# A scaled copy moved from ScalarE to GpSimd in the second of four serial scans, and a reordered tail

## The reference

```python
def step(prev, cur):
    new = cur + jax.nn.relu(_row_conv(prev, K))   # 9 taps along the row, 64 -> 64 channels
    return (new, new)
y = _dir_scan(y, k_td, reverse=False)
y = _dir_scan(y, k_dt, reverse=True)
yt = jnp.swapaxes(y, 1, 2)
yt = _dir_scan(yt, k_lr, reverse=False)
yt = _dir_scan(yt, k_rl, reverse=True)
```

## Time and profile before

| | |
|---|---|
| median of 3 runs | 705.79 us (705.42 to 707.0) |
| the profiled execution | 706.54 us |
| its span, first to last instruction | 704.7 us |
| mean granted clock of TensorE | 0.974 of full speed |
| TensorE busy, matmuls | 636.4 us, 90% |
| VectorE busy | 570.4 us, 81% |
| ScalarE busy | 462.6 us, 66% |
| GpSimd busy | 140.8 us, 20% |
| second scan | 120.6 to 237.0 us of the span |
| attention and tail | from 451 us on |

### The profile page before, as it was taken

How to read it: one execution, slowest core, us unless ns; L and a number is a source line. 1 busy time by engine, 2 the same in 40 slices (tenths; PEclk the granted TensorE clock), 3 DMA queues, 4 the chain that set the end, 5 groups by cost and what they waited for, 6 DMA issues and landing times.

```text
span 704.7 us, 27312 instructions
## 1 busy us (share of the span) xinstructions
PE 636.4 (90%) x10484; PEld 538.4 (76%) x10484; DVE 570.4 (81%) x1943; ACT 462.6 (66%) x1061; POOL 140.8 (20%) x115
## 2 busy tenths in 40 slices
PE   4999999999999899999999999698888898898960
PEld 4899999898888899999999999556454464554530
DVE  4899998888888798989999999897595686785682
ACT  3555666999999666666666666574666676676531
POOL 0023000000000000000000000000627658549363
PEclk9999999999999999999999999889999999999995
DMA  9999850000000000000000000002342835835756
GB/s 175 203 201 198 166 108 1 1 0 0 0 0 0 1 2 0 0 0 0 1 1 0 0 0 0 0 2 60 71 106 57 171 85 104 178 74 122 159 87 120
DMA packets 63611, 43.27 MB, mean 61 GB/s; under 512 B 42000, under 2 KB 56144, under 8 KB 63568
## 3 DMA queue, kind: packets, MB, share of 16 engines
q1 hardware_dynamic: 60272, 41.89, 30.1%
q10 hardware_dynamic: 3296, 0.82, 0.6%
HBM read 33.39 MB, written 9.31 MB: 61 GB/s over the span
## 4 chain that ended last, share of the span: by engine, by line
DVE 31%; PE 26%; issue 17%; POOL 12%; ACT 7%; DMA 3%; DVEq 1%; ACTq 1%; POOLq 0%; SPq 0%
PE bank L468 20%; DVE scan_rows L735 9%; POOL rows_h L395 9%; DVE parts L721 8%; DVE parts L735 7%; DVE fin L794 3%; ACT cols_w L1077 3%; POOL fin L424 2%; DMA rows_h<-bounce 2%; ACT parts L1061 2%; DVEq L735 1%; PE bank L597 1%; DMA yn<-L_conv_k_td 1%; PE bank L518 1%; PE bank L544 1%
## 5 line engine op out<-in xcount | busy, mean ns | idle before, releaser
L468 PE MATMUL bank<-parts 128*128 128x124 f16 (+2 forms) x7560 | 433.5, 219 | 16.1 <-DVE parts L236 8.7
L468 PEld LDWEIGHTS bank<-parts 128*128 128x128 f16 x7560 | 417.7, 98 | 31.8 <-issue 12.0
L1061 ACT ACTIVATE parts<-parts 128x128 f16<-128x128 f16 x508 | 157.1, 309 | 125.9 <-DVE parts L735 104.3
L721 DVE TENSOR_TENSOR parts<-scan_rows,parts 128x128 f16<-128x128 f32 x508 | 149.4, 294 | 14.2
L735 DVE SCALAR_TENSOR_TENSOR parts<-bank,cols_w 128x128 f16<-128x128 f32 x378 | 109.5, 290 | 19.9 <-PE bank L468 4.7
L735 DVE SCALAR_TENSOR_TENSOR scan_rows<-bank,cols_w 128x128 f32<-128x128 f32 x378 | 105.7, 280 | 0.1
L395 POOL TENSOR_TENSOR rows_h<-rows_h 128x512 f32<-128x512 f32 x56 | 81.9, 1495 | 73.4 <-DMA rows_h<-bounce 73.4
L384 POOL TENSOR_TENSOR scale<-dev,half 128x2 f32<-128x2 f32 (+1 forms) x2 | 2.1, 1038 | 412.0 <-DVE dev L819 412.0
L1077 ACT ACTIVATE cols_w<-scan_rows 64x256 f32 (+1 forms) x128 | 82.7, 646 | 2.3
L861 DVE SCALAR_TENSOR_TENSOR kp<-ex,bank 128x512 f32<-128x512 f32 x64 | 40.8, 679 | 43.4 <-ACT ex L1155 42.4
L1069 ACT ACTIVATE cols_w<-scan_rows 128x256 f32 x126 | 52.5, 417 | 5.7 <-DVE scan_rows L735 0.3
(11 more groups left out here) (133 smaller groups left out, 549.2 us busy)
## 6 DMA issues: line engine op xcount, KB each, us to landing
rows_h<-bounce SPq DMA_DIRECT2D x56, 256.0 KB, 5.0
cols_w<-x SPq DMA_DIRECT2D x12, 896.0 KB, 13.8
out<-fin SPq DMA_DIRECT2D x12, 512.0 KB, 7.7
cols_w<-x SPq DMA_DIRECT2D x6, 640.0 KB, 10.8
cols_w<-x SPq DMA_DIRECT2D x6, 256.0 KB, 7.2
out<-rows_h SPq DMA_DIRECT2D x6, 256.0 KB, 4.7
bounce<-recip SPq DMA_DIRECT2D x14, 64.0 KB, 3.3
out<-rows_h ACTq DMA_DIRECT2D x2, 256.0 KB, 6.5
```

Of the source, the lines that this page charges most:

```text
L468: last = nc.tensor.matmul(conv_rows[g][u % SLOTS][:, :, to], w[:, k, d, :], rows_16[:, u % SLOTS, g * GB:(g + 1) * GB, of], start=part_n = ...
L721: nc.vector.tensor_tensor(low[:, slot, gb, :], state[:, slot, gb, :], high[:, slot, gb, :], ALU.subtract).then_inc(low_ready[g], 1)
L1061: act.activation(high_down[:, slot, gb, :], high[:, slot, gb, :], ACT.Copy, scale=1.0 / LOW_SCALE).then_inc(down_ready[g], 1)
```

## The change: what it does

In the second scan GpSimd makes the scaled high part of group 1, with a tensor_scalar of its own for each of the 63 steps, in a new function `second_scan_down`; ScalarE makes that of group 0 alone. VectorE waits for GpSimd's part of two steps before at group 1's high part (the slot is then free), and for the last one before the third scan.

In the tail: the sums of the last image go to the bank `key_ps[0]` and come ahead of other waits; ScalarE copies chunk 1 of the image before the last (`collect`) after it has gathered the last sums, no longer before; `reciprocals_back(0)` goes ahead of `one_before_last(2)`, and VectorE normalises two units before the third statistics; ScalarE does the affine of the image before the last after two of the four copies of the last image; GpSimd makes the last scale after one quarter of the residual, no longer after three; the last shift is made by VectorE; the two halves of the last image have semaphores of their own.

```diff
+            def second_scan_down(slot, row):
+                gb = slice(GB, B)
+                pool.wait_ge(high_ready[1], row)
+                settled(pool)
+                nc.gpsimd.tensor_scalar(high_down[:, slot, gb, :], high[:, slot, gb, :], 1.0 / LOW_SCALE, None,
+                                        ALU.mult).then_inc(down_ready[1], 1)
+
+            with pool.Fori(0, STEPS // BODY) as n:
+                for u in range(BODY):
+                    second_scan_down((u + 1) % SLOTS, n * BODY + (65 + u))
...
             pool.wait_ge(tail_read, 6)
             scale_and_shift(B, 0)
-            for q in range(3):
+            residual(0)
+            pool.wait_ge(tail_read, 8)
+            scale_of_output(B + 1, 1)
+            for q in (1, 2, 3):
                 residual(q)
-            pool.wait_ge(tail_read, 8)
-            scale_and_shift(B + 1, 1)
-            residual(3)
...
+            pe.wait_ge(acc_read, B)
+            pe.wait_ge(kp_ready, KBANKS * B)
+            sums(key_ps[0]).then_inc(tail_done, 1)
+            pe.wait_ge(tail_read, 1)
+            pe.wait_ge(qp_ready, UNITS * B)
             pe.wait_ge(small_read, small_step(B - 1, 5))
             pe.wait_ge(proj_read, NCHUNK * (B - 2) + 2)
-            pe.wait_ge(acc_read, B)
-            sums().then_inc(tail_done, 1)
-            pe.wait_ge(tail_read, 1)
-            pe.wait_ge(qp_ready, UNITS * B)
             for m in range(2):
                 last_denominators(m)
...
+            pe.wait_ge(back_loaded, 16)
+            reciprocals_back(0)
             one_before_last(2)
-            pe.wait_ge(back_loaded, 16)
-            pe.wait_ge(kp_ready, KBANKS * B)
-            reciprocals_back(0)
...
                 if k == 2:
                     dve.wait_ge(saved, 128)
+                    dve.wait_ge(down_ready[1], 127)
...
                             dve.wait_ge(conv_done[g], s + (base + u + 1))
+                            if k == 1 and g == 1:
+                                dve.wait_ge(down_ready[1], s + max(base + u - 1, 1))
...
+                for u in (0, 1):
+                    last_normalised(u)
                 stats_before_last(2)
-                for u in range(4):
+                for u in (2, 3):
                     last_normalised(u)
...
                 dve.wait_ge(scale_ready, 2 * (B + 1))
+                nc.vector.tensor_scalar(shift2[:, 1:2], dev2[:, 3:4], scale2[:, 1:2], norm[:, 3:4], ALU.mult, ALU.add)\
+                    .then_inc(affine_ready, 1)
...
                 dve.wait_ge(last_affine, 1)
-                dve.wait_ge(last_ready, 1)
...
-                    down((u + 1) % SLOTS, n * 6 + (65 + u), lambda: scatter(1, u - 1, n=n))
+                    down((u + 1) % SLOTS, n * 6 + (65 + u), lambda: scatter(1, u - 1, n=n), (0,))
                     scatter(0, u, n=n)
...
-                    collect(b - 1, 1 - par, (0, 1))
+                    collect(b - 1, 1 - par, (0,) if isinstance(b, int) and b == B - 1 else (0, 1))
...
             def tail():
                 gathered(B)
+                collect(B - 2, 0, (1,))
                 affine(B - 1, 1, slice(0, J))
...
                     act.activation(proj[:, 1, chunk_of(i)], last_ps[i][:, :], ACT.Copy).then_inc(last_read, 1)
-                for rows in HALVES:
-                    affine(B, 0, rows)
+                    if i == 1:
+                        for rows in HALVES:
+                            affine(B, 0, rows)
```

More of the change, by code:

```diff
@@ L211, in build @@
         last_stated = sem("last_stated")
-        last_out, last_read, last_sum, last_affine, last_ready = (sem("last_out"), sem("last_read"), sem("last_sum"),
-                                                                  sem("last_affine"), sem("last_ready"))
+        last_out, last_read, last_sum, last_affine = (sem("last_out"), sem("last_read"), sem("last_sum"),
+                                                      sem("last_affine"))
+        last_ready = [sem(f"last_ready{h}") for h in range(2)]
         proj_done, proj_read = sem("proj_done"), sem("proj_read")
@@ L358, in _ @@
             for h, rows in enumerate(HALVES):
-                sp.wait_ge(last_ready, h + 1)
+                sp.wait_ge(last_ready[h], 1)
                 store(B - 1, rows, fin_tail[:, 1], (0,))
@@ L396, in normalise_units, with scale_of_output @@
                                             ALU.mult).then_inc(normed, 1)
-            def scale_and_shift(b, par):
+            def scale_of_output(b, par):
                 nc.gpsimd.tensor_tensor(scale2[:, par:par + 1], dev2[:, 1:2], half[:, 0:1], ALU.pow)\
@@ L404, in scale_and_shift @@
                                         ALU.mult).then_inc(scale_ready, 1)
+            def scale_and_shift(b, par):
+                scale_of_output(b, par)
                 at_least(pool, scale_ready, 2 * b)
@@ L551, in gather, with sums @@
                 last.then_inc(acc_used, 1)
-            def sums():
+            def sums(to):
                 for d in range(2):
-                    nc.tensor.matmul(small_ps[:, 0:P], acc_s[:, d * P:(d + 1) * P], part[:, :],
+                    nc.tensor.matmul(to[:, 0:P], acc_s[:, d * P:(d + 1) * P], part[:, :],
                                      start=d == 0, stop=d == 1)
-                return nc.tensor.matmul(small_ps[:, P:2 * P], w_v[:, :], acc_g[:, :], start=True, stop=True)
+                return nc.tensor.matmul(to[:, P:2 * P], w_v[:, :], acc_g[:, :], start=True, stop=True)
             def group_sums(v):
@@ L571, in small @@
                     at_least(pe, acc_read, b)
-                    last = sums()
+                    last = sums(small_ps)
                 if n == 2:
@@ L993, in tail @@
                 dve.wait_ge(tail_done, 1)
-                nc.vector.tensor_tensor(den_w[:, :], small_ps[:, 0:P], head_of, ALU.mult)
-                nc.vector.tensor_tensor(kv[:, :], small_ps[:, P:2 * P], same_head, ALU.mult).then_inc(tail_read, 1)
+                nc.vector.tensor_tensor(den_w[:, :], key_ps[0][:, 0:P], head_of, ALU.mult)
+                nc.vector.tensor_tensor(kv[:, :], key_ps[0][:, P:2 * P], same_head, ALU.mult).then_inc(tail_read, 1)
                 stats_before_last(0)
@@ L1030, in tail @@
                 dve.wait_ge(last_affine, 1)
-                dve.wait_ge(last_ready, 1)
                 nc.vector.tensor_tensor(fin_tail[:, 1, second, :].rearrange("p j w -> p w j"), mine(second),
-                                        cols[:, :, B - 1, second], ALU.add).then_inc(last_ready, 1)
+                                        cols[:, :, B - 1, second], ALU.add).then_inc(last_ready[1], 1)
             for i in range(NCHUNK):
@@ L1054, in _, with down @@
             load_weights(act, 0, k_td)
-            def down(slot, n, between=lambda: None):
-                for g in range(GROUPS):
+            def down(slot, n, between=lambda: None, groups=(0, 1)):
+                for g in groups:
                     gb = slice(g * GB, (g + 1) * GB)
@@ L1091, in _ @@
                 for u in range(6):
[L1092 removed]
+                    down((u + 1) % SLOTS, n * 6 + (65 + u), lambda: scatter(1, u - 1, n=n), (0,))
                     scatter(0, u, n=n)
             for u in range(STEPS - STEPS % 6, STEPS):
[L1095 removed]
+                down((u + 1) % SLOTS, 65 + u, lambda: scatter(1, u - 1), (0,))
                 scatter(0, u)
@@ L1200, in tail @@
                 act.activation(fin_tail[:, 1, first, :], fin_tail[:, 1, first, :], ACT.Identity, bias=shift2[:, 1:2],
-                               scale=1.0).then_inc(last_ready, 1)
+                               scale=1.0).then_inc(last_ready[0], 1)
                 for h, rows in enumerate(HALVES):
-                    act.wait_ge(last_ready, h + 1)
+                    act.wait_ge(last_ready[h], 1)
                     dst = out[B - 1:B].rearrange("o c (j d) w -> d (o c) j w", d=2)[1]
```

## The result

The changed kernel takes 708.34 us (median of 8, 707.62 to 709.9) against 706.93 for the kernel before (median of 8, 705.08 to 707.82). The ratio is 1.0025, with a 95% interval of 1.0013 to 1.0037: slower by 1.4 us, where +12 was forecast. The direction and the place were right. The size in the second scan was not.

The account below looks back on a forecast made before the run. Group 1's serial loop was taken to bound the second scan, 1.84 us a step rising to 2.14: +18.6, −0.3 at the scan's end, −4 in the tail, +14.3 on 706.5 giving 720.8, forecast as 719; range 703 to 729.

Parts of the forecast that it names:

- The budget of 0.91: Second scan, group 1: the loop gets shorter only if GpSimd's scaled part comes within 0.91 us of the high part's start.
- the 0.93 that stays: Second scan, group 1: from the scaled part's end through TensorE to the next high part, 0.93 us, unchanged.
- GpSimd's start: Second scan: GpSimd begins 0.49 or 0.50 us after the high part's start, 0.29 for that part plus 0.20 for waiting.
- its price: Second scan: GpSimd's tensor_scalar on 128 elements takes 0.48 us, with ends 0.25 and 0.60.
- the other user of its operands' path: Second scan: GpSimd meets VectorE's two-input low part, loses the near tie, and delivers 1.14 us after the high part's start.
- The row at 524.40: Profile row used as evidence: a GpSimd instruction started 0.01 us ahead of a two-input VectorE one, yet ended 1.13 after it.
- one more wait: Second scan: VectorE's added wait ahead of group 1's high part costs up to 0.08 us a step, taken as 0.07.
- rival 1: Second scan: GpSimd wins the tie, step 1.98 us, +8.7 there, total +4.4, 711 us; chance 0.17.
- The signs: Wrong if GpSimd's instructions take under 0.4 us, start within 0.15, never meet low parts, or the tail's last end moves under 2.
- rival 2: Second scan: GpSimd's operation is as quick as a cast, 0.25 us; 697 with the tie won, 707.5 lost; chance 0.16.
- The tail: End of the kernel: four edits to the path that sets the end gain 4 us, with ends −1 and −6.7.
- the collision: Tail: two VectorE instructions and three GpSimd residual pieces want one path, 7.5 us in a row, ending 693.6 instead of 696.88.

Follow-up runs that it names:

- constant waits: Changed kernel with GpSimd's 63 steps written out, so each waits on a constant without a semaphore of its own in between: 704.5 us, ratio 0.9956.
- copy: Changed kernel with a GpSimd tensor_copy in place of the multiplication by 1/256: 694.43 us in one execution.
- two inputs: Changed kernel with GpSimd's tensor_scalar replaced by a tensor_tensor of high minus high: 699.82 us in one execution.
- later start: Changed kernel with one more semaphore raised by GpSimd before each of its 63 instructions, so they start behind VectorE's low part: 720.7 us in one execution.
- the tail part alone: Kernel before with only the change's tail edits, its second scan left as it was: 702.88 us, ratio 0.9947.
- The last experiment: Changed kernel with VectorE making group 1's scaled part, and last image's stores ahead of the second half of the image before: 692.93 us; old store order 694.24.
- the kernel without the wait: Changed kernel without VectorE's added wait for the scaled part of two steps before: 710.21 us in one execution.
- with VectorE: Changed kernel with group 1's scaled part of the second scan made by VectorE instead of GpSimd: 694.51 us, ratio 0.9813 to the kernel before.

## Why the prediction was right or wrong

**The bound and the loop: right.** The budget of 0.91, the 0.93 that stays, and the rule that a step is 0.93 plus the time from high part to scaled part held in five kernels, to 0.03 us. That time was 1.01 (changed kernel), 0.90 (constant waits), 0.75 (copy), 0.87 (two inputs) and 1.20 (later start), and the steps were 1.95, 1.84, 1.71, 1.81 and 2.13. The sum gives 1.94, 1.83, 1.68, 1.80 and 2.13.

**GpSimd's start: right; its price a little low.** The start came at 0.48, for 0.49 to 0.50. The instruction took 0.528, for 0.48, which is 3 us over 62 steps.

**The step that failed** is the one called "the other user of its operands' path", where I wrote "I expect it to lose: result at 0.81 + 0.48 − 0.15 = 1.14". It won. The result came at 1.01, and the 0.13 us are 8 us over 62 steps. The term itself was further off: with its real price a losing instruction would have ended at 0.81 + 0.53 − 0.15 = 1.19, as with the later start it did (1.20). So winning was worth 0.18 us a step, 11 us, and the dearer instruction took 3 of them back. I had a lead of 0.02 to 0.03 from sums of rounded rows, and set it against a single row with a lead of 0.01. The real lead was 0.04. The row at 524.40 is the only near tie of that kind in the trace that I had, and it turned out to be the exception. Outside the second scan the twelve traces have 35 pairs in which a GpSimd cast or tensor_tensor and a VectorE low part or L258 (the instruction of that row) start within 0.15 us of each other. In 34 of them the one that started first took its own time, to 0.05 us; the row at 524.40 (0.011 ahead) is the 35th. The smallest lead with which GpSimd won was 0.006 where it followed its own last instruction without a pause, and 0.032 where it started from idle as it does in the scan. The latter is this row of the changed kernel, where the low part takes 0.83:

```profile
45.82 0.72 POOL L237 CAST parts<-yn 128x640 f16<-128x640 f32 x1 [43.28 <-DMA yn<-L_conv_k_dt]
45.85 0.83 DVE L737 TENSOR_TENSOR parts<-scan_rows,parts 128x128 f16<-128x128 f32 x1
```

The sum turns on the sign of a difference smaller than its own rounding: 0.08 us later the same kernel is 12 us slower. Such a term should have been carried as two cases of about the same chance, with a forecast that says so, and not as one with three times the chance of the other. The page "SBUF — State Buffer" of the Trainium skill, section "Who interferes with whom", says that the order of issue decides who blocks. That agrees with the row at 152.07, with the later start and with the 34 pairs; only the lead of 0.01 at 524.40 goes against it. That the first has the shared pair for the whole instruction the same section says of VectorE's modes that use both ports, and the forecast took it for this pair of instructions as well. The traces bear that out for GpSimd's copy, cast and two-input instruction, but not for its tensor_scalar: the low part was held up by 0.10 beside one that went on for another 0.49, and not at all when it began 0.15 behind it.

**The second step that failed** is "one more wait", taken at 0.07: measured nothing, another 4 us. I had read group 0's longer way as the price of a second wait. By the trace it is that of a wait that comes after the late one in the queue: in the third scan of the kernel before, group 0's high part starts 0.18 us after VectorE's queue passes the wait for the matmuls (at 253.64), with a second wait between, and group 1's 0.11 after its own (at 252.82), with none. The new wait comes before the late one. No run moved a wait behind the late one to test this.

Together 0.20 us a step, 12.4 us. The second scan was to lose 18.6 and lost 6.6; rival 1, with +8.7, was the case that came. Without the 0.07 and with the real price it would have said 0.93 + 0.50 + 0.53 = 1.96, and 1.94 with the measured start.

**The signs.** None of those by which the forecast said that it would be wrong came: the instructions took 0.53, started 0.19 after the high part's end and always had low parts beside them, and the last instruction moved by 4.1. They could not tell who wins the tie. What hung on a step of 2.14 did not come: TensorE was busy for 93% of the scan and not 80%, and ScalarE was free for a fifth of it and not a third. The lower end of the range, 703, also lies below the case that it was said to be, rival 2 with the tie lost, which the forecast put at 707.5.

**The end of the scan**: −0.3 was expected. From group 1's last high part to the third scan's first it was 4.04 us before and 3.47 after, −0.6. But the other kernels had 3.46 to 4.08, the copy 4.07 and the tail part alone 3.83, so this one difference shows little.

**The tail: right in sum.** −4 expected, −4.1 timed alone. By its terms: until the last statistics −1.0 (expected −1.2; from the last key matmuls to VectorE's first statistics of the last image 15.05 and 14.01 us); at the last instruction −4.1 (expected −3.3), with the collision in its place; but the stores after it took 1.0 longer, where I had counted on 0.7 less. The last experiment points to where that went: stores of the last image stood behind GpSimd's last piece, and the other order gave 1.2 to 1.3 back.

**What stays open.** The first scan, which no kernel changed, took 108.6 to 111.0 us in the traces (from its first high part to that of the second scan), so a difference of a single execution has an error of about 2 us in it; the timed ratios do not hang on one, but the later start, the copy, the kernel without the wait and the two-input one were timed once each, and there the steps and not the times carry the argument. What keeps some steps at 1.75 instead of 1.64 with VectorE was not tried, nor where 3 of the 6.4 us of the constant waits went.

## What to carry to other kernels

In a loop of dependent steps, write the loop as one sum and count the budget of the piece that is moved, from its input to its result: an idle engine helps only if start and instruction together fit in it, and the start on GpSimd behind a semaphore that it raises itself was 0.19 us here where ScalarE's was 0.03. Before giving work to a slow idle engine, ask whether a busy but fast one has room: VectorE, busy for 1.5 of 1.84 us, did in 0.18 what GpSimd did in 0.53, and that was worth 13.8 us. Where two engines come to the same operands within some hundredths of a microsecond, carry both outcomes, and if the kernel is to stay so, move one of them away from the tie.

## What the runs showed of the hardware that I had not expected

- A tie of 0.04 us between a GpSimd and a two-input VectorE instruction decides 0.11 us for GpSimd each time, and it falls the same way step after step: 62 of the 63 low parts beside GpSimd were stretched in the changed kernel, none with the later start.
- How long the winner holds the other up depends on its operation. Beside a GpSimd copy, cast or two-input instruction that came first, the low part (0.29 alone) ended 0.14 to 0.15 us after it. Beside the tensor_scalar of 0.53 us one that came 0.04 later ended 0.10 before it, and one that came 0.15 later was not held up. By an estimate from these rows the tensor_scalar let go 0.29 us after its start (0.04 + 0.39 − 0.145), which is as long as the copy takes.
- On GpSimd, 128 f16 elements in each of 128 partitions cost 0.29 us to copy, 0.40 to subtract and 0.53 to multiply by a constant. The operation with one input and a constant is dearer than the one with two inputs.
- VectorE's multiplication by a constant, 0.18 us alone, added nothing to the time between its neighbours' starts (0.52 with and without).
